# Another written-out order for the score, value and side work of a macaron layer's attention phases

## The reference, cut to what matters

```python
x = L0_attn_x                                    # (8, 512, 128)
x = x + 0.5 * ffn(layernorm(x))                  # relu(x W1q^T + b1) W2q^T + b2
x = x + attn(layernorm(x))                       # q, k rotated, softmax(q k^T / sqrt(8)) v, then Wo
x = x + 0.5 * ffn(layernorm(x))                  # the same weights again
```

## Time and profile before

| | |
|---|---|
| median of 3 runs | 584.28 us (583.87 to 587.52) |
| the profiled execution, its own time | 578.99 us |
| its span in the profile | 577.2 us |
| TensorE busy | 518.6 us, 90% of the span |
| VectorE busy | 396.2 us, 69% |
| ScalarE busy | 369.8 us, 64% |
| GpSimd busy | 220.6 us, 38% |
| TensorE's granted clock, mean | 0.994 |
| first e / end of the last pv, from the span's start | 69.02 / 558.50 us |

### The profile page before, as it was taken

One profiled execution on the slowest core, in us unless ns is written; L12 is line 12 of the kernel. 1 busy time (PEld: TensorE's weight loads), 2 busy tenths in 40 slices (PEclk: granted clock), 3 DMA queues, 4 the chain that ended last, 5 costly groups with the idle time before them and its releaser, 6 DMA issues.

```text
span 577.2 us, 8687 instructions
## 1 busy us (share of the span) xinstructions
PE 518.6 (90%) x3230; PEld 237.4 (41%) x3230; DVE 396.2 (69%) x579; ACT 369.8 (64%) x432; POOL 220.6 (38%) x291
## 2 busy tenths in 40 slices
PE   6659999889999999999999888989899989898986
PEld 4446635233535344343535233423334333432346
DVE  4874976767786687657776687668856776678314
ACT  4669675677475765767475666576566657576751
POOL 1554372527342546427340545153613531103202
PEclk9998999999999999999999999999999999999999
DMA  7056038012800344012800362034502360000000
GB/s 226 30 182 147 1 112 219 2 29 100 204 1 20 111 132 92 2 46 101 203 1 21 111 162 60 2 112 131 110 1 57 148 147 2 21 1 3 2 18 19
DMA packets 19177, 44.60 MB, mean 77 GB/s; under 512 B 2624, under 2 KB 5440, under 8 KB 18112
## 3 DMA queue, kind: packets, MB, share of 16 engines
q1 hardware_dynamic: 18464, 43.53, 27.4%
q10 hardware_dynamic: 672, 0.52, 0.3%
HBM read 20.45 MB, written 18.87 MB: 68 GB/s over the span
## 4 chain that ended last, share of the span: by engine, by line
PE 71%; DVE 16%; ACT 4%; DMA 4%; issue 4%; POOL 1%; SPq 1%; POOLq 0%; DVEq 0%; ACTq 0%
PE heads_acc L556 20%; PE unit L541 13%; PE unit L526 12%; DVE maxima L837 10%; PE side L611 9%; PE side L605 5%; PE side L594 3%; DMA q_stack<-max_T 3%; ACT hidden L737 2%; PE heads_acc L619 2%; PE unit L611 1%; PE side L590 1%; PE side L599 1%; PE side L575 1%; DVE attn_out L850 1%
## 5 line engine op out<-in xcount | busy, mean ns | idle before, releaser
L837 DVE TENSOR_REDUCE maxima<-unit 128x2 f32<-128x1024 f32 x256 | 307.1, 1221 | 129.9 <-PE unit L526 129.7
L747 ACT ACTIVATE probs<-unit 128x1024 f32<-128x1024 f32 x256 | 261.5, 1025 | 128.1 <-PE unit L541 126.8
L541 PE MATMUL unit<-q_stack,k_stack 64*128 64x512 f32 x512 | 125.6, 488 | 25.1 <-DVE maxima L837 18.8
L556 PE MATMUL heads_acc<-probs,v_heads 128*32 128x512 f32 x1024 | 136.4, 605 | 1.0 <-ACT probs L747 1.0
L526 PE MATMUL unit<-k_stack,q_stack 62*128 62x512 f32 x512 | 115.9, 448 | 0.0
L526 PEld LDWEIGHTS unit<-k_stack,q_stack 62*128 62x128 f32 x512 | 48.2, 184 | 104.8 <-issue 87.6
L541 PEld LDWEIGHTS unit<-q_stack,k_stack 64*128 64x128 f32 x512 | 47.7, 183 | 91.2 <-DVE maxima L837 43.1
L1001 POOL TENSOR_SCALAR max_parts<-maxima 128x16 fp32r<-128x16 f32 x32 | 6.6, 205 | 192.7 <-DVE maxima L837 192.7
L611 PE MATMUL side<-w_q,hidden 128*128 128x128 f32 x416 | 59.3, 287 | 0.0
L611 PEld LDWEIGHTS side<-w_q,hidden 128*128 128x128 f32 x416 | 50.1, 191 | 15.5 <-issue 14.6
L737 ACT ACTIVATE hidden<-side,b_col 128x512 f32<-128x512 f32 x49 | 33.8, 690 | 18.1 <-PE side L605 18.1
(11 more groups left out here) (142 smaller groups left out, 472.4 us busy)
## 6 DMA issues: line engine op xcount, KB each, us to landing
k_scratch<-k_parts SPq DMA_DIRECT2D x16, 512.0 KB, 2.9
q_scratch<-q_parts SPq DMA_DIRECT2D x16, 512.0 KB, 2.9
k_stack<-k_scratch SPq DMA_DIRECT2D x14, 512.0 KB, 7.1
q_stack<-q_scratch SPq DMA_DIRECT2D x14, 512.0 KB, 9.0
resid<-in_x SPq DMA_DIRECT2D x8, 256.0 KB, 6.9
k_swap<-k SPq DMA_DIRECT2D x16, 128.0 KB, 2.3
q_swap<-q SPq DMA_DIRECT2D x16, 128.0 KB, 2.3
out_y<-resid SPq DMA_DIRECT2D x7, 256.0 KB, 2.0
```

The costliest lines, as they stand in the source:

```text
L541: mm = pe.matmul(to[:, e, :], k_stack[part, quad // NQ % 2, pair, kt * P:(kt + 1) * P], q_stack[part, quad // NQ % 2, pair, :], start=True ...
L556: mm = pe.matmul(heads_acc[32 * j:32 * j + 32, :], v_heads[:, b % 2, at, ODD * odd:ODD * odd + 32], probs[:, burst % RING, j, :], start=(k ...
L747: act.activation(probs[:, burst % RING, 2 * pp:2 * pp + 2, :], unit_of(USE_OF["exp", n]), ACT.Exp, scale=SCALE).then_inc(s_exp, 1)
L837: dve.tensor_reduce(maxima[:, quad % 2, :, r], unit_of(USE_OF["max", k]), AX_X, ALU.max).then_inc(s_max, 1)
```

## The change

Only the two plan strings change; no function does. The exponential and maxima pairs, which alternated with side work or a burst after every one or two, now stand in runs of two to six. The bursts pv no longer stand behind every second e, and the side pieces stand in other rows. The two first rows of each plan, before and after:

```diff
 PE_FIRST = """
-e m attn_T@1
-e m k@1
+attn_T@1 k@1 e m m q@1
+e
...
 PE_STEADY = """
-e m ffn1_T
-e pv m ffn1_up0
+ffn1_T m e
+heads_copy1@-1 m pv ffn1_up0 e m ffn1_up1
...
```

More of the change, by code:

```diff
@@ L55 @@
 PE_FIRST = """
-e m attn_T@1
-e m k@1
[L58 to L71, removed]
-e m
-e pv m
-heads_copy0 e m
-e pv m heads_T0
-e m
[L77 to L87, removed]
+attn_T@1 k@1 e m m q@1
+e
+e
+e m m ffn1_T m pv
+e
+e ffn1_up0 ffn1_stats@5 pv m m pv max_T1 m ffn1_up1 m
+e ffn1_up2
+e
+e m m ffn1_up3
+e
+e attn_stats
+e m pv ffn1_down0 ffn1_down1 pv m m
+e ffn1_down2
+e ffn1_down3
+e max_T2 m
+e pv m m pv
+heads_copy0 pv m v m e
+e m
+e
+e pv
+e m pv max_T3 m
+e attn_T
+e
+e pv heads_T0
+e m
+e
+e m m k pv m
+e m pv
+e m m
+e pv max_T4 m
+e q m pv m
+e
 """
 PE_STEADY = """
-e m ffn1_T
-e pv m ffn1_up0
[L92 to L104, removed]
-e pv m
[L106 to L119, removed]
+ffn1_T m e
+heads_copy1@-1 m pv ffn1_up0 e m ffn1_up1
+e m
+e ffn1_stats@5 heads_T1@-1
+e pv m
+e m max_T1 pv ffn1_up2 m
+e m out_T pv ffn1_up3 m
+e
+e out
+e ffn2_stats
+e pv m m ffn1_down0 ffn1_down1 ffn1_down2 m
+e m ffn1_down3 pv
+e max_T2
+e m pv m
+e attn_stats
+e v
+heads_copy0 pv m m pv ffn2_T e m ffn2_up0
+e
+e m ffn2_up1
+e pv heads_T0
+e m m ffn2_up2
+e pv max_T3
+e m m ffn2_up3 pv
+e m ffn2_down0
+e m m ffn2_down1 ffn2_down2 ffn2_down3
+e m
+e pv attn_T
+e m
+e k pv
+e m m pv max_T4
 e m q
-e pv m
+e m pv
 """
```

## The result

The changed kernel takes **544.95 us** (median of 4 runs, 544.44 to 550.48) against 584.08 (4 runs, 578.63 to 587.52): a ratio of **0.938**, with a 95% interval of 0.928 to 0.948. The forecast was 549.3 us, with a range of 542 to 575. Medians here are of all executions; ratios leave out those that ran over 1.5% above the fastest of their kernel, at a lower granted clock.

What follows compares the result with a forecast made beforehand. The loop was taken to run at TensorE's pace, losing time to runs of pairs and waits. Savings of 21.4 us (runs) and 15.5 (waits), less 1.9 for bursts behind full work, took 35.0 off 584.28: 549.3 us, range 542 to 575.

Steps and rivals of the forecast that it cites:

- Runs, -21.4: On TensorE, each run of neighbouring score pairs (exponential or maxima) costs 0.20 us; 311 runs become 204, 21.4 us off.
- Full work next to pv, +1.9: On TensorE, 38 values bursts right behind full-array work cost 0.05 each, +1.9 us, between bounds of -3.8 and +3.8.
- The walk: Start-by-start reckoning of each phase's new order on TensorE, VectorE and ScalarE; 60.1 us for a phase with both FFN halves.
- Waits, 54 to 39: TensorE's waits over all phases fall from 54 to 39 us, 15.5 us off.
- the up projection of the second half: ffn2's first up projection, phases 1 to 7: waits for x_lo, starting 2.05 us after the transposes, 0.80 of it wait.
- attn_out and the max row: Waits that go away: attn_out before up projections (0.8 us, 10 times) and four long ones for the max row's DMA.
- the ring's waits in phase 4: Three score units are too few where runs fall together: waits of 0.49 + 0.36 + 0.31 and 0.52 + 0.50 + 0.90 us.
- The sum, 35.0: Whole kernel: phases 36.9 us shorter (21.4 runs, 15.5 waits), with +1.9 for bursts behind full work, a gain of 35.0 us.
- The waits stay as they are: Rival: TensorE's waits stay at 54 us, so only runs less the burst term count, 19.5 off, 564.8 us; chance 0.14.
- Pairs of maxima hold the ring: Rival: 50 maxima pairs directly before another wait for their unit, 0.7 us each, 35 us come back, 584 us; chance 0.12.
- Bursts on their own exponentials: Rival: 32 values bursts with one or no spare exponential ahead wait 1.4 us each, 45 us, giving 594 us; chance 0.08.

Runs made afterwards that it cites:

- e1: Kernel before, with the maxima pair put ahead of the values burst wherever a burst had pairs on both sides; 575.21 us, 0.984 of the kernel before.
- e5: Changed kernel, with bursts that stood between full work and a pair moved one pair into the run, 30 runs more; 559.25 us, 0.960 of the kernel before.
- e4: Changed kernel, with the third maxima transpose of phases 1 to 7 moved nearer its first exponential, behind heads_copy0; 570.15 us, 0.978 of the kernel before.
- e4b: Changed kernel, with the third maxima transpose moved nearer its first exponential but ahead of heads_copy0, so its copy is free; 548.72 us, 0.941 of the kernel before.
- e0: The changed kernel itself, unedited, measured once more; 547.27 us, 0.940 of the kernel before.

## Why the prediction was right, point by point

**Runs, -21.4: right.** The trace has 204 runs from the first e to the last burst, where the one before has 311. Two equal pairs take 0.66 as forecast, e1 measured 2.55 for 14 runs and e5 1.05 for 5: 0.18 and 0.21 a run. (The 20.2 us that TensorE is busy less are near the forecast too, but they hold a dip of the clock and the joined down projections, L611 59.3 to 53.8, so they do not measure the runs alone.)

**Full work next to pv, +1.9: wrong, it is 0.** The transposes take 0.59 up to a burst and 0.58 up to a pair; 0 lies between the bounds of -3.8 and +3.8, and half of the nearest row's cost was the wrong pick.

**Full work next to full work: not in the sum, -4.1.** The walk took full work's own time to be the same in both orders (its 57.7 for a phase with both halves has the 37.6 of the old order). But down projections that stand together take 0.19 less per place where two meet, 4.1 us in all. The Trainium skill, "TensorEngine Tiling (Array Packing)", Key Properties, says that a change of the tiling mode drains TensorE. The runs agree for the two kinds measured: a run of pairs pays 0.20 on top of its pairs, a row of down projections 0.19 on top of its matmuls. A burst behind full work is such a change too, and the transposes pay for it what they pay for a pair.

**Waits, 54 to 39: right in direction, too large.** The phases gained 35.5 at a full clock. Less 21.4 for runs and 4.1 for joined full work, 10.0 are left for waits, and 15.5 were forecast. In phases 2 and 3 the own time is then 57.7 - 2 x 0.39 = 56.9, and 59.6 leaves 2.7 of waits, where the walk had 2.4. (What of the phases TensorE was not busy fell from 37.6 us, 492.97 less 455.38, to 24.0, 458.71 less 434.75. That 13.6 is not the fall of the waits, since a matmul's recorded length runs past the next one's start.) By item: the up projection of the second half was put at 2.05 after the transposes, with 0.80 of wait, and starts 2.16 after them, which by the starts is 0.91 (the bracket has 0.83); attn_out and the max row went as said; the ring's waits in phase 4 were put at 0.49 + 0.36 + 0.31 and 0.52 + 0.50 + 0.90 and are 0.49 + 0.41 + 0.26 and 0.40 + 0.63 + 0.99. Phases 1 to 3 came out at 60.40, 59.60 and 59.63 (forecast 60.1), 4 and 5 at 55.50 and 55.52 (55.2), 6 and 7 at 54.01 and 54.12 (53.7 and 53.8). Phase 0 was put at 54.4 behind the fill of 3.49 us (65.53 to 69.02), 57.9; it takes 58.71. In all 457.5 against 456.1.

**The sum, 35.0: right, in part by luck.** At a full clock the phases gained 492.97 - 457.5 = 35.5. Of its terms only the runs came out as put: the 4.1 that the walk did not see and the 1.9 that a burst does not cost made up for 5.5 too much taken off the waits. The forecast of 549.3 is 4.4 above the median since it was taken from the median of before; by the profiled executions it was 544.0 against 545.37. Both medians move by several us with the clock, so this part is scatter and no step.

**The rivals.** *The waits stay as they are*: waits fell, so no. *Pairs of maxima hold the ring*: waits for maxima are 9.2 us and not above 18.8, so no; yet e1 shows the ring as a real price, for another neighbourhood (in e m e m the second m waits for probs, 23.2 us, in place of the 18.8). *Bursts on their own exponentials*: a burst waits for probs twice, 1.1 us in all, as before (1.0), so no.

**What was not in the working.** That a copy named in a plan has its place on ScalarE's list and can block it was given as the walk's assumption ("a side copy is never later than its engine's list makes it") and not as a price. e4 measures it: 2.1 to 2.7 us a phase at a full clock, and 23 us in the median, for one name on the wrong side of another.

## What to carry to other kernels

Where small matmuls use the array in another tiling than the rest, price each run of them, and each row of full work between them, by start-to-start distances and not by busy shares, and join both; but pairs only so far as the buffers drain behind them: e1 kept half of what its runs saved, and e5 lost nearly as much in waits as its 30 runs cost. When a piece of work is moved in an order that several in-order engines share, look up what stands ahead of it on each of them: one copy behind a waiting one cost, by the phases, nearly half of this change's gain. A transfer that is late for its reader can be given more work to hide behind, which works here. A place further from other traffic may help as well; e4b fits that, but does not prove it.

## What the runs showed of the hardware

TensorE's clock falls in the middle of the loop, with the engine busy. The windows around such a dip after the change (the column behind POOL is the granted clock):

```profile
360.00:383.00 23.00, 21.12 (x138) 8.21 (x134) 20.50 (x28) 16.09 (x19) 13.19 (x15) 1.00 0.52 154
383.00:386.50 3.50, 3.50 (x19) 1.09 (x15) 1.57 (x2) 2.08 (x3) 3.39 (x6) 0.54 0.98 211
386.50:416.00 29.50, 28.36 (x195) 13.26 (x191) 21.39 (x29) 20.18 (x25) 7.43 (x12) 1.00 0.10 24
```

In these 3.5 us the mean granted clock is 0.54, so the engine stands at the lower of its two levels (1.2 instead of 2.4 GHz) most of that time, though it had been busy for 21.12 of the 23 us before at the full one. A phase with one such dip is 1.2 to 1.3 us longer (56.74 against 55.52; 56.82 against 55.50), and which phases have one differs from run to run: one here, three in e0. The part ahead of the first maxima transpose varies as well, 66.14 us here and 68.87 in e0, at a mean clock of 0.87 and 0.83. Over ten runs of the changed kernel the time follows the mean clock: 544.1 to 545.4 at 0.98 to 0.99, 549.9 to 550.7 at 0.97. The Trainium skill, "Advanced Engine Details and Errata", Clock Domains, names a gate for an idle array and a power limiter; no run here tells which of them it is, or whether something else.
